# Moving the edges of layer two's attention into its neighbours: first maxima and first expert into layer one, late projections and outputs between the quads

## What is computed

```python
xn = layernorm(x)
x = x + attention0(xn) + lowprec_ffn(xn)   # non-transposed softmax over keys, biases, gelu
xn = layernorm(x)
x = x + attention1(xn) + moe(xn)           # causal softmax, no biases
# moe: for each of 8 experts, acc += (silu(xn @ wg) * (xn @ wu)) @ wd, width 512
```

## Time and profile before

| | us |
|---|---|
| median of 3 runs (1461.59 to 1465.1) | 1464.94 |
| the profiled execution's own time | 1459.96 |
| its span, first to last instruction | 1458.2 |
| busy in it: PE, DVE, ACT, POOL | 1309.7, 1017.8, 825.3, 733.3 |

### The profile page before, as it was taken

How to read it: one execution, slowest core, us unless ns; L and a number is a source line. 1 busy time by engine, 2 the same in 40 slices (tenths; PEclk the granted TensorE clock), 3 DMA queues, 4 the chain that set the end, 5 groups by cost and what they waited for, 6 DMA issues and landing times. The chain is left out here.

```text
span 1458.2 us, 23453 instructions
## 1 busy us (share of the span) xinstructions
PE 1309.7 (90%) x8264; PEld 765.8 (53%) x8264; DVE 1017.8 (70%) x2380; ACT 825.3 (57%) x1236; POOL 733.3 (50%) x853
## 2 busy tenths in 40 slices
PE   3888988989889953999999999999999999999978
PEld 1444444444444422566665666566565665656645
DVE  4566676766767512788787877878787787877843
ACT  1455666666666621565665656656566566656640
POOL 5243464655644544455554655645556555545530
PEclk7799999999999975899999999999999999999997
DMA  5222232423423224110011100100100100000013
GB/s 170 67 79 75 89 110 87 149 86 102 121 77 109 83 67 115 34 48 29 21 48 31 49 30 21 47 31 27 52 27 20 52 27 30 27 31 9 16 38 102
DMA packets 54258, 88.64 MB, mean 61 GB/s; under 512 B 9943, under 2 KB 20700, under 8 KB 54142
## 3 DMA queue, kind: packets, MB, share of 16 engines
q1 hardware_dynamic: 52990, 86.61, 19.0%
q10 hardware_dynamic: 1152, 0.52, 0.2%
HBM read 41.69 MB, written 44.31 MB: 59 GB/s over the span
## 5 line engine op out<-in xcount | busy, mean ns | idle before, releaser
L1143 POOL TENSOR_TENSOR a_h_lo<-a_h,a_h_hi 128x512 fp32r<-128x512 f32 x256 | 328.8, 1284 | 164.1 <-ACT a_h_hi L1190 163.0
L650 DVE TENSOR_REDUCE l_mx<-bank_pair 128x2 f32<-128x1024 f32 (+3 forms) x256 | 203.1, 819 | 129.0 <-PE bank_pair L890 128.2
L1252 DVE SCALAR_TENSOR_TENSOR a_h<-a_h,bank_pair 128x512 f32<-128x512 f32 x256 | 175.4, 685 | 138.9 <-ACT a_h L1186 138.9
L131 PE MATMUL bank_pair<-st 24*128 24x512 f32 (+3 forms) x1024 | 206.1, 388 | 62.2 <-ACT l_E L736 26.7
L166 DVE CUSTOM_DVE_ANT_0 bank_pair<-bank_pair,mask 128x512 f32<-128x512 f32 (+3 forms) x512 | 238.1, 517 | 6.5 <-PE bank_pair L131 6.4
L1190 ACT ACTIVATE a_h_hi<-a_h 128x512 fp32r<-128x512 f32 x256 | 161.6, 631 | 132.2 <-DVE a_h L1258 128.9
L1197 ACT ACTIVATE a_E<-bank_pair 128x1024 f32<-128x1024 f32 (+1 forms) x192 | 169.6, 883 | 115.0 <-PE bank_pair L138 115.0
L736 ACT ACTIVATE l_E<-bank_pair 128x1024 f32<-128x1024 f32 (+1 forms) x192 | 168.4, 879 | 85.6 <-PE bank_pair L138 85.5
L131 PEld LDWEIGHTS bank_pair<-st 24*128 24x128 f32 x1024 | 104.7, 187 | 204.2 <-issue 164.3
L190 POOL TENSOR_SCALAR_AFFINE_SELECT a_E<-a_E 128x256 f32<-128x256 f32 (+1 forms) x192 | 94.7, 493 | 216.1 <-ACT a_E L1197 216.0
L1258 DVE TENSOR_TENSOR a_h<-a_h,bank 128x512 f32<-128x512 f32 x256 | 176.0, 688 | 31.3 <-DVE a_h L1252 6.0
(11 more groups left out here) (133 smaller groups left out, 2199.3 us busy)
## 6 DMA issues: line engine op xcount, KB each, us to landing
st<-stack_d SPq DMA_DIRECT2D x256, 96.0 KB
stack_d<-l_q_k_hi SPq DMA_DIRECT2D x64, 256.0 KB, 3.0
stack_d<-l_q_k_lo SPq DMA_DIRECT2D x32, 256.0 KB, 3.3
o_d<-l_O SPq DMA_DIRECT2D x32, 256.0 KB, 2.1
o_d<-a_O SPq DMA_DIRECT2D x32, 256.0 KB, 2.0
l_at<-o_d SPq DMA_DIRECT2D x8, 256.0 KB, 3.4
l_share<-rden_d SPq DMA_DIRECT2D x8, 256.0 KB, 3.2
a_wst<-wg_in SPq DMA_DIRECT2D x8, 256.0 KB, 2.8
```

What stands on the lines that cost most here:

```text
L131: return nc.tensor.matmul(bank[:, col:col + w], st[rows, 0, bass.ts(t, P)], st[rows, 1, 0:w], start=first, stop=last)
L650: ins = nc.vector.tensor_reduce(out, pair[:, :, col:col + width(kb)], AX.X, ALU.max)
L1143: nc.gpsimd.tensor_tensor(h_lo[:, q % RH, :], h[:, q % RH, :], h_hi[:, q % RH, :].bitcast(F32), ALU.subtract).then_inc(h_lo_ready, 1)
L1252: nc.vector.scalar_tensor_tensor(hq, hq, 1.0, g_bank[:, :], ALU.add, ALU.mult).then_inc(silu_ready, 1)
```

## The change

1. `layer0` has steps -7 .. 32. The scores, maxima and maxima rows of "quad 32", which is quad 0 of layer two, are made in step 31, its stack and two more are loaded in layer one, and its maxima are added at step 32.
2. Expert 0 is loaded at step 22 and split at the ends of steps 24, 26 and 28 (one ACT copy and one POOL subtraction each); expert 1 is loaded at step 29. `sel_setup` (POOL) moves from step 32 to step 25.
3. What steps 33 to 38 did goes into the loop of `attend_moe`: a table `LATE` gives 16 of the 32 quads one unit each (X, Q, K, V of batches 6 and 7, and A, the output projection, of layer one's batch 7 and of layer two's batches 0 to 6). PE does it right behind `maxima_rows`, in the second of the two score banks; ACT (X, Q, K, V) or DVE (A) reads it, and the next quad's first scores wait for that. The row sums are inverted on DVE one quad ahead, stored and loaded again as shares by SP, and divided on POOL in unit 1 of the odd step.
4. `attend_moe` has no preamble; `acc` is written by the first expert and not cleared.
5. `finish` has only batch 7's attention left; for the others it only adds `acc` to xs. Four banks are used for the sums.
6. In layer one's `scores_and_keys` PE issues T's first blocks, then waits for S's banks, then issues S's first blocks.
7. POOL's splits of the experts and the loads of experts 2 to 7 lie in other units of the loop; buffers that both blocks use are allocated once; a DMA scratch size is 8192.

The core of the diff:

```diff
-    for g in range(FIRST, QUADS + 7):
+    for g in range(FIRST, QUADS + 1):
-            put(("S", g + 1, n), 0 <= g + 1 < QUADS)
+            put(("S", g + 1, n), 0 <= g + 1 <= QUADS)
@@ layer0, sync
+                if g == SPLIT_AT[0] - 2:
+                    load_expert(sp, wst, experts, 0, expert_in)
+                if g == SPLIT_AT[2] + 1:
+                    sp.wait_ge(expert_lo, 3)
+                    load_expert(sp, wst, experts, 1, expert_in)
@@ layer0, gpsimd (scalar has the copy to w_hi in the same steps, last in the step)
-                if g == QUADS:
+                if g in SPLIT_AT:
+                    m = SPLIT_AT.index(g)
+                    pool.wait_ge(expert_hi, m + 1)
+                    nc.gpsimd.tensor_tensor(w_lo[:, m, :], wst[:, m, :], w_hi[:, m, :].bitcast(F32), ALU.subtract).then_inc(expert_lo, 1)
+                if g == SEL_AT:
                     sel_setup()
@@ layer0, tensor, scores_and_keys
-                    begin("S", g + 1, n)
                 for k in range(2):
-                    for r in range(HALVES):
-                        if more and k < len(score_blocks):
-                            scores(nc, pair_of("S", g + 1, n)[:, r, :], stacks[(g + 1) % STACKS], r, n // 3, score_blocks[k], k == 0, False)
                     for r in range(HALVES):
                         if here and k < len(key_blocks):
                             ins = keys_by_queries(...)
+                    if more and k == 0:
+                        begin("S", g + 1, n)
+                    for r in range(HALVES):
+                        if more and k < len(score_blocks):
+                            scores(...)
@@ attend_moe
+LATE = {0: ("X", 6), 1: ("A", 0), 2: ("X", 7), 3: ("Q", 6), 4: ("K", 6), 5: ("A", 1), 6: ("V", 6), 7: ("Q", 7), 8: ("K", 7), 9: ("A", 2),
+        10: ("V", 7), 13: ("A", 3), 17: ("A", 4), 21: ("A", 5), 25: ("A", 6), 29: ("A", 7)}
@@ attend_moe, sync, per quad g
+                if due[0] == "A":
+                    store_rden(due[1])
                 if g > 0:
                     sp.wait_ge(O_copied, g)
                     store_outputs(sp, o_d, O, g - 1, o_out[(g - 1) % 2])
+                if due[0] == "A":
+                    load_share(due[1])
+                if coming[0] == "A" and coming[1] > 0:
+                    load_attention(coming[1])
+                if done[0] in ("Q", "K"):
+                    store_parts(*done)
@@ attend_moe, vector
+                if not odd and done[0] == "A":
+                    add_attention(done[1])
+                    if odd and n == 2 and coming[0] == "A":
+                        invert(coming[1])
+                    if not odd and n == 1 and done == ("A", 0):
+                        statistics()
@@ attend_moe, gpsimd: lo of X, Q, K in unit 0 of the next even step; divide in unit 1 and normalize in unit 0 of the odd step
@@ attend_moe, tensor
+                    if g > 0:
+                        pe.wait_ge(mrow_ready, g)
+                    if g - 1 in LATE:
+                        pe.wait_ge(late_read, LATE_TURN[LATE[g - 1]])
                     if odd and n == 3 and more:
                         maxima_rows(g + 1)
+                        if g in LATE:
+                            late_unit(*LATE[g])
+            def late_unit(kind, b):
+                if kind == "X":
+                    ...                                  # 4 transposes of xn
+                elif kind == "A":
+                    pe.wait_ge(atT_ready, b + 1)
+                    ...                                  # 4 matmuls at x wo
+                elif kind == "V":
+                    ...                                  # 4 matmuls xnT x wv
+                else:
+                    ...                                  # one matmul of 512 columns
+                ins.then_inc(late_ready, 1)
@@ finish, tensor
+            for b in range(4):
+                sums(b)
             pe.wait_ge(rden_ready, 1)
+            spread(nc, share_bank, sel, rden, last).then_inc(share_ready, 1)
+            for b in range(4, last):
                 sums(b)
+            pe.wait_ge(atT_ready, 1)
+            sums(last)
```

More of the change, by code:

```diff
@@ L347, in steps @@
         def steps():
-            for step in range(-7, QUADS + 7):
+            for step in range(FIRST, QUADS + 1):
                 yield step, step // QUADS_A_BATCH, step % QUADS_A_BATCH
@@ L1123, in _ @@
                     sp.wait_ge(T_ready, UNITS_A_QUAD * g)
-                    load_stacks(sp, stacks, st_d, g - 1 + STACKS, stack_in[(g - 1) % STACKS])
+                    if (g + 3) // QUADS_A_BATCH >= 6:
+                        sp.wait_ge(parts_out, 4 * LATE_STORES)
+                    load_stacks(sp, stacks, st_d, g + 3, stack_in[(g + 3) % STACKS])
+                done, due, coming = (LATE.get(quad, ("", 0)) for quad in (g - 1, g, g + 1))
+                if due[0] == "A":
+                    store_rden(due[1])
@@ L1164, in _ @@
                     lo(NC * i + n)
-                    if n < 3 and b == 1 and x + 1 < EXPERTS:
-                        split(x + 1, n)
+                    if (b, n) in SPLIT_LO and x + 1 < EXPERTS:
+                        split(x + 1, SPLIT_LO.index((b, n)))
+                    if not odd and n == 0 and done[0] in ("X", "Q", "K"):
+                        rest_of_late(*done)
+                    if odd and n == 1 and due[0] == "A":
+                        divide(due[1])
+                    if odd and n == 0 and due == ("X", 7):
+                        normalize()
         @block.scalar
@@ L1218, in _ @@
                     hi(NC * i + n)
+                    if odd and n == NC - 1 and g in LATE and LATE[g][0] != "A":
+                        read_late(*LATE[g])
                     if not odd and n == NC - 1 and g > 0:
@@ L1355, in down @@
                     ins.then_inc(acc_ready, 1)
-            pe.wait_ge(pv_set, 1)
-            for n in range(UNITS_A_QUAD):
-                scores_and_keys(-1, n, None)
-            maxima_rows(0)
             for i in range(STEPS):
@@ L1414, in _, with add @@
         def _(dve):
+            def add(b):
+                x_b = xs[:, bass.ts(b, N)]
+                dve.wait_ge(sum_ready, b + 1)
+                nc.vector.tensor_tensor(x_b, sum_banks[b % 4][:, :], x_b, ALU.add).then_inc(y_ready, 1)
+            for b in range(3):
+                add(b)
             dve.wait_ge(den_in, 16)
@@ L1433, in _ @@
-            add(B - 1)
+            add(3)
+            dve.wait_ge(at_in, 16)
+            dve.wait_ge(share_ready, 1)
+            nc.vector.tensor_tensor(atT[:, :], at[:, :], share_bank[:, :], ALU.mult).then_inc(atT_ready, 1)
+            for b in range(4, B):
+                add(b)
         @block.tensor
         def _(pe):
-            def share(b):
-                if b > 1:
-                    pe.wait_ge(atT_ready, b - 1)
-                spread(nc, share_banks[b % 2], sel, rden, b).then_inc(share_ready, 1)
@@ L1442, in sums @@
             def sums(b):
-                pe.wait_ge(atT_ready, b + 1)
-                if b > 1:
-                    pe.wait_ge(y_ready, b - 1)
+                if b > 3:
+                    pe.wait_ge(y_ready, b - 3)
                 for t in range(NT):
-                    o = sum_banks[b % 2][:, bass.ts(t, D)]
-                    nc.tensor.matmul(o, acc[:, bass.ds(b * N + t * P, P)], ident[:, :], start=True, stop=False)
-                    ins = nc.tensor.matmul(o, atT[:, b % 2, bass.ts(t, P)], wo[:, :], start=False, stop=True)
@@ L1450, in sums @@
-                ins.then_inc(ao_ready, 1)
-            pe.wait_ge(w_in, 16)
+                    o = sum_banks[b % 4][:, bass.ts(t, D)]
+                    ins = nc.tensor.matmul(o, acc[:, bass.ds(b * N + t * P, P)], ident[:, :], start=True, stop=b < last)
+                    if b == last:
+                        ins = nc.tensor.matmul(o, atT[:, bass.ts(t, P)], wo[:, :], start=False, stop=True)
+                ins.then_inc(sum_ready, 1)
+            for b in range(4):
+                sums(b)
```

359 lines of the change are left out of this document (234 added, 125 removed).

## The result

| | before | changed |
|---|---|---|
| median, us | 1463.26 (1455.95 to 1465.1, 4 runs) | 1383.20 (1377.35 to 1384.35, 4 runs) |
| ratio, 95% interval | | 0.9466 [0.9447, 0.9485] |
| profiled execution, own time | 1459.96 | 1377.35 |
| its span | 1458.2 | 1375.6 |

A forecast was written before the change was run, and what follows sets the result against it. Dependencies bound 104 us at block edges, PE's nearly full queue the loop. 1459.96 - 53.9 + 3.0 + 1.7 + 0.5 - 4 + 14.7 + 4 - 19 = 1407.0, with 5.0 carried over 1412 us; 8-in-10 range 1398 to 1426.

The forecast's parts named there:

- T's blocks first in layer one: Layer one: PE gains only where the awaited exponential was itself late; -4 us, bounds +2 to -24.
- rival 2: Layer one: earlier exponentials also free ACT for later ones, 20 of 24 us of waits go; 1396 us, chance 0.10.
- layer one shorter by more than 10 us: Layer one: listed among the signs that would show the prediction wrong.
- The gap before the loop: Between layer one and the loop: first gate_up at 533.7 instead of 587.58; -53.9 us, bounds -54.4 to -50.7.
- What was put into layer one: Layer one: quad 32's units in step 31 +3.0, expert 0's splits +1.7, one more load +0.5 us.
- The late units and DVE: Loop: 16 late units cost +14.7 us (+8 to +26); DVE's statistics and inversions +4 (+1 to +12).
- The small additions: Loop, DVE: additions of DEN_EPS may each wait for a whole POOL low part through the shared port lock.
- rival 1: Loop: port lock felt, each of 8 inversions waits 1.1 us, +9 instead of +2; 1419 us, chance 0.14.
- rivals 3: Loop: late units cost double as copies and unit add up, 16 x 1 us more; 1428 us, chance 0.12.
- 4: Loop: PE waits in order for a late divide, making the kernel slower; 1482 us at 10 us late, chance 0.03.
- 5: Block edge: loop can't start until some late work is in, part of 53.9 stays; 1432 us at 20, chance 0.03.
- The last block: End of kernel: 21.5 us instead of 40.5; -19 us, bounds -16 to -21.

The follow-up runs named there:

- s_first: Changed kernel with the old order in layer one, S's wait and S's first blocks ahead of T's; 1404.81 us, ratio 0.9611.
- combined: Changed kernel without the negated maxima's low part, batch 6's normalization moved to the second block, last block's sums and reciprocal earlier; 1349.60 us, ratio 0.9242.
- waits_together: Changed kernel with T's first blocks still first, but the wait for S's banks ahead of both; 1400.39 us, ratio 0.9586.
- fill_half: Changed kernel with about half of the filler matmuls in layer one; 1394.73 us.
- fill_none: Changed kernel with no filler matmuls in layer one; 1425.59 us.
- before_pad: Kernel before with one VectorE memset ahead of the loop cut into eight, seven more instructions; 1457.18 us, ratio 0.9959.
- neg_drop: Changed kernel without VectorE's second instruction (L185) for the low part of the negated maxima; 1360.63 us, ratio 0.9325.

## Why the prediction was wrong, step by step

**T's blocks first in layer one: the step that failed.** The forecast was -4, measured are -15.7 (profile, s_first against changed); the medians differ by 21.6. The kernel before with this edit alone gives -14.2 and -15.6. The text said: "S still waits just as long for the same exponential, and PE takes its work in order, so PE gains only where the exponential waited for was itself late." The first half overlooks that the wait was not only S's: with S's wait ahead of both, T's own matmuls stood behind it and came after it. Now they fill it, T's exponential starts earlier, and so the next wait is shorter too: ACT's next exponential is what S waits for. 20.6 of the 24.0 us of the earlier trace rows went. That was rival 2, given 0.10, which had 20 of the 24 us go: its mechanism was right, its chance not, and its price of 16 us more than the forecast's too high (measured 11.7 more), since T and S gave up running side by side. The bound of -24 was on the page, and the value near the other end was taken from one place of 0.26 us instead of from the row that groups all 49. The smaller part of the error, some 4 to 5 us, is the clock: the profile before had four steps of 16.2 us beside like ones of 14.6, and the prediction took no account of them. Each has a wait of 1 us with the clock at half behind it, and costs 1.6 us. The changed kernel's profiled execution has none of these, and that is in part luck: the same order in other kernels has one to three, behind shorter waits (combined: 15.7, 16.2 and 15.3 us). The forecast had named "layer one shorter by more than 10 us" as a sign of being wrong, and it came: layer one's last output is at 511.83 instead of 525.88.

**The gap before the loop: right.** From layer one's last output to the first `gate_up` it was 61.7 us and is 7.75: -54.0 for -53.9. The switch of blocks took 0.35.

**What was put into layer one: priced too dear.** Step 31 takes 12.5 us with the old order (forecast 13.1 with the maxima rows). s_first, which has all of it, reaches its last output at 527.98 instead of 525.88: +2.1 for +5.2. Step 29 is 1.1 us shorter in it than in the kernel before (15.1 for 16.2), because the clock did not fall there; without that it would be +3.2.

**The late units and DVE: +11.4 for +14.7 and +4.** Corrected for VectorE's stalls, the quads give A 0.61, V 0.62, Q 0.84, K 0.84, X 0.8 for batch 6 and 0.1 for batch 7, and 1.53 for A(0). Forecast were 0.93 for A and V: the slack was 0.3 rather than 0.06, read from one place; where in the chain it lies was not followed. X of batch 7 is so cheap in a quad in which L185 was not held, and that alone was worth 0.6 elsewhere. X of batch 6 lies in the stretch from the first `gate_up` to the first output, 39.8 us long; it is 41.3 in s_first, where the clock is low for 8.3 us from the first `gate_up` on instead of 3.2, so some 1.6 us of the miss here are this execution's. In A(0)'s quad the statistics lie too, so the 0.9 above the other A's may be theirs (forecast +1); no run parts them. The inversions on DVE cost nothing (quads ahead of an A are as short as others). Seven of the eight reciprocals start within 0.01 us of a low part and are not held by it; they have one input. The small additions, for which the forecast feared the lock, had ended before POOL's low part began, so the trace does not test them:

```profile
L1419 DVE RECIPROCAL a_rden<-a_den 128x64 f32<-128x64 f32 x8 | 4.4, 552 | 0.2
L1417 DVE TENSOR_SCALAR a_den<-a_den 128x64 f32<-128x64 f32 x7 | 1.3, 185 | 0.0
```

So rival 1 fell, as rivals 3 (double price), 4 (late divide: no wait of PE for it, the shares land in 3.3 us) and 5 did. PE's longest wait for a late unit to be read was 0.64 us, once, behind X of batch 6.

**VectorE's stalls: -3.6, not in the sum.** 13 before and 2 after, 0.33 us each. Nothing in the change means it: this is luck. 11.4 - 3.6 = 7.8, as the marks show.

**The last block: -22.4 for -19**, beyond the bound of -21. The clock was up from the first sums on (8 instructions in about 1.0 us instead of 1.7), so DVE's three additions ended at 3.7 us instead of 6.2, and the reciprocal at 7.4 instead of 10.1. From there to the end it took 10.7 us, between the 9.1 and 14.1 of the forecast. The chain was priced right and the clock guessed wrong for this execution. The same last block takes 20.8 us in the profiled executions of waits_together, fill_half and fill_none, with a clock of 0.75 in it instead of 0.91; there the forecast's 21.5 would have been near, so part of this term is luck too:

```profile
1376.27:1397.10 20.83, 14.28 (x74) 12.41 (x74) 9.76 (x11) 0.00 (x0) 0.00 (x0) 0.75 0.42 127
```

**Sum.** -11.7 (order of T and S) -3.6 (the rest of layer one) -7.3 (late units and DVE) -3.6 (stalls) -3.4 (last block) = -29.6. The terms are differences of the same marks, so they must add up; the experiments bear out the first, the stalls and the price of the late units.

## What to carry to other kernels

A wait that stands ahead of two pieces of work costs both; before pricing a reordering at nothing, ask for each instruction behind the wait whether it needs what is waited for, and take the sum of the waits of that line as the bound rather than one example as the measure. Then take off what the two pieces gave each other: here 28 us of idle time went and 16 us of time, because matmuls that had run side by side now follow each other. Read the step lengths for outliers: a step that is longer than its like at a lower clock is lost time beside the waits, and whether it comes varies from one execution to the next. And a small instruction with an odd duration (1.2 us for 16 columns) is worth removing even where the shown waits behind it are a fifth of its time (8.0 of 36.8 us).

## What had not been expected of the hardware

- VectorE lost 0.46 us in the same place of every second quad, and seven more instructions ahead of the loop took all 13 of these away (before_pad). With fewer instructions to a quad (neg_drop) there are 6, 207 recorded instructions apart, or exactly 256 with the waits for semaphores counted.
- Removing one instruction of 1.2 us from VectorE gave 0.6 us in each quad in which it had been held beside POOL, and nothing in the one quad in which it had not, though PE's waits for VectorE came to 0.26 a quad.
- The same instruction was held to the end of a POOL instruction with two inputs (30 of 30 times) and not held beside one with a single tensor as input (0.20 us).
